# A decoder block on one core: the first sum of a job postponed, products cut into single pieces, and 26 of 64 steps plain instead of 30 in the last six jobs

## The chip, the core and the metric

The kernel runs on one core of a Trainium2 chip. The metric is the device time of one execution in microseconds (us); lower is better. The engines are called as in the profile: PE (TensorE, with PEld for its weight loads), DVE (VectorE), ACT (ScalarE), POOL (GpSimd) and SP (SyncE, which here only issues transfers).

## What is computed

A decoder block over 8 rows of 256 positions and 256 features, all in f32: two Mamba layers, cross attention, and a mixture of 8 experts of which each position uses 2. A layer norm closes each of the three. The two Mamba layers take most of the time. Their core is a recurrence over the positions, for 512 channels and 64 states each:

```python
def step(h, inp):
    u_t, dt_t, B_t, C_t = inp
    dA = jnp.exp(dt_t[:, :, None] * A)
    h = h * dA + (dt_t * u_t)[:, :, None] * B_t[:, None, :]
    y = jnp.einsum('bds,bs->bd', h, C_t)
    return (h, y)
...
combine = combine.at[jnp.arange(T)[:, None], topk_idx].set(topk_scores)
h = jax.nn.relu(jnp.einsum('td,ehd->teh', xf, w1) + b1)
expert_out = jnp.einsum('teh,edh->ted', h, w2) + b2
```

## The kernel before

A *job* is one Mamba layer of one row: 16 jobs, in the order of `JOBS` (row 0's first layer, then alternately the first layer of row b and the second of row b-1, at the end the second layer of row 7). A *step* is one of the 64 states of a job: all 512 channels (4 times 128 partitions) by 256 positions at once. There are 1024 steps, one after the other, and each passes four engines:

- PE fills `psX[i % 2]` with the input of step i (`fill_x`), after scan i-2 has left that buffer.
- ACT makes the decays `dA` with four exponentials (L1311).
- DVE runs the scan (L1343), a recurrence over 1024 elements, into `h`.
- POOL multiplies `h` by C (L1098) into `hC`, of which there are three.
- PE adds the result to `psY` with eight transposing matmuls (`sum_states`, L1656), two steps after (`LAG = 2`).

`KINDS` gives each step one of three ways to make its input. *Plain* (P): PE spreads b with 2 matmuls (L1619), and DVE multiplies by `dtu` in PSUM ahead of the scan (L1333). *Rows scaled* (T): ACT scales rows of `dtuT` (L1282) and PE turns them with 8 matmuls (L1627). *By matrix* (M): PE multiplies `dtuT` with a diagonal matrix in 16 matmuls (L1637); SP stores the diagonal nine steps ahead and loads the matrix five steps ahead. So P costs DVE an instruction, T costs ACT two, and M costs PE the most. Jobs 1 to 9 follow `EARLY` (22 P, 21 M, 21 T), jobs 10 to 15 follow `LATE`.

When the 64 states of a job are summed, DVE multiplies `psY` with the gate (`gate`, L1358), and only then may the first sum of the next job overwrite `psY`. In iteration i the instructions stand in this order: on PE `fill_x(i + 1)`, the sum of step i-2, then small work; on DVE the gate (where step i-2 is the first of a job), the multiplication of step i+1 if plain, the scan of step i+1.

*Small work* is all the rest: the projections, convolution and softplus of the next job, `turn` and `next` or `proj` behind the gate (L1762, L1595), attention, routing, and the experts in 53 tiles of 128 slots (`x_turn`, `hid` at L1595, `out` at L1682). The class `Schedule` plans it once, when the program is built: it keeps a model time for each engine, and after each step's own work `fill` takes tasks out of four chains (`chains`, rank 0 the next job, 1 a row's attention and routing, 2 experts, 3 outputs) as long as they end before `latest` says that the next fill, decay or product is due. A task is put at a step, `beside[i]`, and each engine does its pieces of `beside[i]` in that order. The first `WINDOW` tasks of each chain are looked at. A product of four matmuls is two tasks here (`z` and `z+`, `2 * MM` each), a fourth of a `hid` half is one of 448 ns. DVE takes small work only ahead of a plain step. Where the expert chain has nothing and room is left, `keep_busy` puts in `keep` pieces: `KEEP` = 4 times `TURN` = 109 ns of room is taken for each idle transpose (L1881). Whatever is not placed by the last step goes into `tail`; the experts of the last group (15 tiles, rows 6 and 7) always do, since row 7 must be routed first.

The planner's model of the sum does not wait for the gate.

Of the kernel before, what the change touches and what calls it, by code (L numbers as in the profile page):

```python
# [20 lines left out]
P = 128  # L21
# [31 lines left out]
LATE = "PTPMPTPTPMTPTPT" * 4 + "PTPM"  # L53
# [19 lines left out]
def kind_of(i):  # L73

    return KINDS[i] if 0 <= i < STEPS else PLAIN

# [33 lines left out]
WINDOW, FIRST, LONG, HOP = 24, 1500, 3300, 60  # L110
# [15 lines left out]

def task(name, n, part, eng, ns, *needs, opens=None, frees=None):
    return Task((name, n, part), eng, ns, needs, opens, frees)

# [11 lines left out]
def tasks_pre(n):  # L141
# [5 lines left out]
    if n >= 2:  # L147
        before = (("next+", n - 2, 1),) if JOBS[n - 2][0] == 0 else (("proj+", JOBS[n - 2][1], 1),)
    gates, out = [], []
    for tc in range(KL):  # L150
        gates += [task("z", n, tc, "PE", 2 * MM, *src, *((("u+", n, 1),) if n == 0 else ()), opens="G"),
                task("z+", n, tc, "PE", 2 * MM, ("z", n, tc)),
                task("z_copy", n, tc, "ACT", EVICT, ("z+", n, tc), frees=("z", n, tc))]
    if n > 0:
        out += gates
    for half in range(2):
        out += [task("u", n, half, "PE", 2 * MM, *src, *before, opens="G"),
                task("u+", n, half, "PE", 2 * MM, ("u", n, half))]
        if n == 0 and half == 1:
            out.append(task("conv", n, half, "DVE", 3600, ("u+", n, half), frees=("u", n, half)))  # L160
            continue
        for j in range(TAPS):
            needs = [("u+", n, half)]
# [9 lines left out]
    if n == 0:  # L173
        out += gates
    out += [task("silu", n, 0, "ACT", 4800, ("z_copy", n, 1), ("add_tap", n, (1 if n else 0, TAPS - 1)), *(() if n else (("conv", 0, 1),))),
            task("c", n, 0, "PE", 2 * MM, ("silu", n, 0), opens="G"),
            task("c+", n, 0, "PE", 2 * MM, ("c", n, 0)),
            task("c_copy", n, 0, "ACT", 400, ("c+", n, 0), frees=("c", n, 0)),
            task("b", n, 0, "PE", 8 * TURN, ("silu", n, 0), opens="G"),
            task("b+", n, 0, "PE", 8 * TURN, ("b", n, 0)),  # L180
            task("bT_copy", n, 0, "ACT", 330, ("b+", n, 0), frees=("b", n, 0))]
    for half in range(2):
        chain = (("log", n, 0),) if half else ()
        out += [task("dt", n, half, "PE", 2 * MM, ("c_copy", n, 0), opens="G"),
                task("soft", n, half, "ACT", 2 * EVICT, ("dt", n, half), *chain, frees=("dt", n, half)),
# [14 lines left out]
def tasks_post(n):  # L200
# [6 lines left out]
    if l == 0:  # L207
        out += [task("next", n, 0, "PE", 2 * MM, *copied, opens="G"),
                task("next+", n, 0, "PE", 2 * MM, ("next", n, 0)),
                task("next", n, 1, "PE", 2 * MM, ("next+", n, 0)),  # L210
                task("next+", n, 1, "PE", 2 * MM, ("next", n, 1)),
                task("next_copy", n, 0, "ACT", EVICT, ("next+", n, 1), frees=("next", n, 0))]
    else:
        out += [task("proj", b, 0, "PE", 2 * MM, *copied, opens="G"),
                task("proj+", b, 0, "PE", 2 * MM, ("proj", b, 0)),
                task("proj", b, 1, "PE", 2 * MM, ("proj+", b, 0)),
                task("proj+", b, 1, "PE", 2 * MM, ("proj", b, 1)),
                task("resid1", b, 0, "DVE", 2350, ("proj+", b, 1), frees=("proj", b, 0)),
                task("rstd", b, 0, "POOL", 900, ("resid1", b, 0)),
                task("norm1", b, 0, scaler(b), 780, ("rstd", b, 0))]  # L220
# [3 lines left out]
def tasks_kv(b):  # L224

    out = []
    for name, before in (("k", ("score+", b - 1, 0)), ("v", ("av+", b - 1, 0))):
        out += [task(name, b, 0, "PE", 2 * MM, *((before,) if b else ()), opens="G"),
                task(name + "+", b, 0, "PE", 2 * MM, (name, b, 0)),
# [4 lines left out]
def tasks_row(b):  # L234
# [7 lines left out]
    if b > 0:  # L242
        last.append(("b2_add", b - 1, 0))
# [1711 lines left out]
```

## Time and profile before

| | |
|---|---|
| time, median of 3 runs | 3259.71 us (3256.25 to 3264.41) |
| the profiled execution | 3258.22 us |
| its span, first to last instruction | 3256.4 us |
| its granted TensorE clock, mean | 0.970 |
| first scan to last scan | 35 to 3041 us |
| the last six jobs | 1854 to 3041 us |
| after the last scan | 215 us |

How to read it: each engine works from its own queue in order, and "idle" is the time in front of an instruction in which its engine did nothing; the name behind the arrow is what ended that. A group is all instructions of a line, engine and shape; its busy time is a union, the mean is that of one. PE's ends are modelled, so that matmuls behind each other overlap a little; the distance between the starts of two groups tells what a group costs PE.

### The profile page before, as it was taken

What the parts mean: (1) busy time and instruction counts of PE and PEld (TensorE: products, weight loads), DVE (VectorE), ACT (ScalarE), POOL (GpSimd) and SP (SyncE); (2) the same over time, 40 slices, a digit from 0 to 9 for tenths busy, and PEclk for the clock granted to TensorE, in tenths of its full rate; (3) what the DMA queues carried; (4) which work ended last, traced back from release to release, by engine and by line L of the source; (5) the groups of instructions that cost most, each with busy time, mean ns of one, the idle gap of its engine ahead of it and who ended that gap; (6) DMA issues with size and microseconds to landing.
All of it is one profiled execution on the core that took longest, in us unless ns stands there. A gap on an engine that the chain in (4) does not pass through costs nothing.

```text
span 3256.4 us, 59741 instructions
## 1 busy us (share of the span) xinstructions
PE 2873.5 (88%) x21945; PEld 2614.9 (80%) x21945; DVE 2911.1 (89%) x2039; ACT 2625.0 (81%) x6098; POOL 2661.3 (82%) x1317
## 2 busy tenths in 40 slices
PE   6889899998988899898988799899998989899676
PEld 5888888887878788787878789788888878888466
DVE  6999999999999999999999999999999999999410
ACT  7878888886879788887989699898989879788222
POOL 4989999898989899888989798887888788878401
PEclk8999999999999999999999999999999999999788
DMA  3345442222222222122222235334353335634076
GB/s 113 103 155 172 152 154 65 71 67 70 73 63 64 62 73 75 55 66 72 70 69 63 85 129 166 96 106 156 119 159 102 102 122 163 204 123 141 25 270 210
DMA packets 285448, 358.35 MB, mean 110 GB/s; under 512 B 100554, under 2 KB 180435, under 8 KB 284772
## 3 DMA queue, kind: packets, MB, share of 16 engines
q1 hardware_dynamic: 281202, 343.75, 33.7%
q0 software_dynamic: 3072, 8.39, 0.8%
q8 instruction: 175, 2.87, 0.4%
q10 hardware_dynamic: 882, 2.38, 0.2%
q14 instruction: 117, 0.96, 0.1%
HBM read 303.70 MB, written 50.73 MB: 109 GB/s over the span
## 4 chain that ended last, share of the span: by engine, by line
PE 32%; ACT 21%; POOL 17%; DVE 14%; issue 13%; DMA 2%; SPq 1%; POOLq 0%; DVEq 0%; ACTq 0%
POOL hC L1098 14%; ACT dA L1311 10%; PE psY L1656 9%; DVE h L1343 9%; PE psG L1595 8%; PE psX L1637 4%; ACT xs L1282 3%; PE psG L1682 3%; PE psX L1627 3%; DVE psX L1333 3%; PE psX L1595 2%; ACT gT L1153 1%; PE psX L1619 1%; DMA w_up<-in_w_exp 1%; ACT scratch L1150 1%
## 5 line engine op out<-in xcount | busy, mean ns | idle before, releaser
L1098 POOL TENSOR_TENSOR hC<-h,cb 128x1024 f32<-128x1024 f32 x1024 | 2401.9, 2368 | 376.7 <-DVE h L1343 361.2
L1343 DVE TENSOR_TENSOR_SCAN h<-dA,psX 128x1024 f32<-128x1024 f32 (+1 forms) x1102 | 2300.2, 2124 | 102.3 <-ACT dA L1311 34.0
L1311 ACT ACTIVATE dA<-dt,negA 128x255 f32<-128x255 f32 x4096 | 1722.3, 506 | 167.0 <-DVE h L1343 165.8
L1656 PE MATMUL psY<-ident,hC 128*128 128x128 f32 x8192 | 1087.5, 277 | 53.6 <-DVE gT L1358 39.4
L1656 PEld LDWEIGHTS psY<-ident,hC 128*128 128x128 f32 x8192 | 941.6, 143 | 69.5 <-DVE gT L1358 42.7
L1637 PE MATMUL psX<-diag_b,dtuT 128*128 128x128 f32 x4080 | 514.5, 280 | 52.1 <-DVE h L1343 49.2
L1637 PEld LDWEIGHTS psX<-diag_b,dtuT 128*128 128x128 f32 x4080 | 487.9, 195 | 86.3 <-issue 82.0
L1333 DVE TENSOR_TENSOR psX<-dtu,psX 128x1024 f32<-128x1024 f32 x411 | 497.0, 1209 | 22.2 <-PE psX L1619 21.6
L1627 PE MATMUL psX<-ident,xs 128*128 128x128 f32 x2864 | 382.0, 277 | 108.6 <-ACT xs L1282 66.9
L1282 ACT ACTIVATE xs<-dtuT,bT 128x512 f32<-128x512 f32 x716 | 477.0, 720 | 0.2
L1627 PEld LDWEIGHTS psX<-ident,xs 128*128 128x128 f32 x2864 | 320.6, 142 | 164.3 <-ACT xs L1282 91.1
L1682 PE MATMUL psG<-w_down,hid 128*128 128x256 f32 x692 | 180.2, 384 | 13.3 <-DMA w_down<-in_w_exp 6.1
L1619 PE MATMUL psX<-ident,bT 128*128 128x128 f32 x822 | 163.7, 282 | 15.1 <-DVE h L1343 13.1
L1595 PE MATMUL psG<-xgT,w_up 128*128 128x128 f32 x1216 | 164.8, 278 | 9.5 <-DMA w_up<-in_w_exp 6.0
L1595 PEld LDWEIGHTS psG<-xgT,w_up 128*128 128x128 f32 x1216 | 151.7, 192 | 19.3 <-DMA w_up<-in_w_exp 7.6
L1881 PE MATMUL psG<-ident 128*128 128x128 f32 x985 | 158.3, 273 | 0.0
L1682 PEld LDWEIGHTS psG<-w_down,hid 128*128 128x128 f32 x692 | 119.7, 191 | 31.9 <-DMA w_down<-in_w_exp 10.0
L1619 PEld LDWEIGHTS psX<-ident,bT 128*128 128x128 f32 x822 | 104.4, 141 | 49.0 <-DVE h L1343 26.7
L1881 PEld LDWEIGHTS psG<-ident 128*128 128x128 f32 x985 | 117.6, 141 | 4.8 <-issue 4.1
L1554 DVE SCALAR_TENSOR_TENSOR hC<-got,slot_weight,hC 128x256 f32<-128x256 f32 x8 | 3.7, 483 | 126.0 <-DMA got<-y_slots,slot_of 92.6
L1266 ACT ACTIVATE hid<-psG,b_tile 128x128 f32<-128x128 f32 x304 | 86.0, 370 | 31.5 <-PE psG L1595 31.4
L1054 POOL DMA_INDIRECT got<-y_slots,slot_of x28 | 29.1, 1040 | 92.2 <-DMA y_slots<-yg 86.5
(203 smaller groups left out, 2046.1 us busy)
## 6 DMA issues: line engine op xcount, KB each, us to landing
cb<-c_dram SPq DMA_DIRECT2D x256, 512.0 KB, 4.0
w_up<-in_w_exp SPq DMA_DIRECT2D x173, 256.0 KB, 3.1
w_down<-in_w_exp SPq DMA_DIRECT2D x173, 256.0 KB, 2.8
diag_b<-b_dram SPq DMA_DIRECT2D x255, 128.0 KB, 3.6
x_slots<-got SPq DMA_DIRECT2D x32, 512.0 KB, 5.0
y_slots<-got SPq DMA_DIRECT2D x32, 512.0 KB, 5.0
dA<-in_w_exp SPq DMA_DIRECT2D x39, 256.0 KB, 5.1
h<-in_w_exp SPq DMA_DIRECT2D x39, 256.0 KB, 4.9
```

Of the source, the lines that this page charges most:

```text
L1098: eng.tensor_tensor(hC[i % NHC][:, :, :], h[i % NH][:, :, :], cw.to_broadcast([P, KI, L]), ALU.mult).then_inc(times_c, 1)
L1282: made = eng.activation(xs[:, tc, :], dtuT[n % 2][:, tc, :], ACT.Identity, scale=bT[n % 2][:, tc, s:s + 1])
L1311: made = eng.activation(dA[j % NA][:, c, 1:L], dt[n % 2][:, c, 1:L], ACT.Exp, scale=negA[:, JOBS[n][0], c, s:s + 1])
L1333: eng.tensor_tensor(x[:, :, :], dtu[n % 2][:, :, :], x[:, KI - 1:KI, :].to_broadcast([P, KI, L]), ALU.mult).then_inc(times_b, 1)
L1343: made = eng.tensor_tensor_scan(h[i % NH][:, part, :].rearrange("p c t -> p (c t)"), dA[i % NA][:, part, :].rearrange("p c t -> p (c t)"), ...
L1595: made = eng.matmul(dst, lhs, rhs, start=begin and i == 0, stop=end and i == len(terms) - 1)
L1619: made = eng.transpose(psX[i % 2][:, KI - 1, tc * P:(tc + 1) * P], bT[n % 2][:, tc, s:s + 1].to_broadcast([P, P]), ident[:, :])
L1627: made = eng.transpose(psX[i % 2][:, c, tc * P:(tc + 1) * P], xs[:, tc, c * P:(c + 1) * P], ident[:, :])
L1637: made = eng.matmul(psX[i % 2][:, c, tc * P:(tc + 1) * P], dtuT[i // S % 2][:, tc, c * P:(c + 1) * P], diag_b[k % NDIAG][:, tc, :], start= ...
L1656: made = eng.matmul(psY[:, tc, c * P:(c + 1) * P], hC[i % NHC][:, c, tc * P:(tc + 1) * P], ident[:, :], start=s == 0 and c == 0, stop=s == ...
L1682: made = eng.matmul(bank[k][:, 0:D], hid[half][:, i, :], w_down[slot][:, i % 2, :], start=half == i == 0, stop=half == 1 and i == 3, skip_ ...
L1881: eng.transpose(bank["M"][:, 0:P], ident[:, :], ident[:, :])
```

## The change

Three edits.

1. `sums_at(i)`: the first sum of a job (but for job 0) is not done in iteration i = first step + 2, but in the next one, ahead of that iteration's own sum. The sums stay in the same order. The planner's model has the same.
2. `CUTS` and `cuts`: each product is planned, and may be done, in pieces of one matmul with 256 columns (a `hid` quarter in two of 224 ns, `o` in three per half, `logit`, `b2`, `dt`, `count` in two) instead of two pieces of two. The matmuls are the same and as many. `WINDOW` goes from 24 to 40, since the chains have more tasks.
3. `LATE`: 26 P, 25 T, 13 M instead of 30 P, 25 T, 9 M. The last step of all is P in both, so that the last job goes from 31 P and 8 M to 26 P and 13 M.

```diff
-LATE = "PTPMPTPTPMTPTPT" * 4 + "PTPM"
+LATE = "PTMPT" * 12 + "PTMP"
...
+def sums_at(i):
+
+    j = i - LAG
+    if j < 0 or j >= S and j % S == 0:
+        return ()
+    return (j - 1, j) if j > S and j % S == 1 else (j,)
...
-WINDOW, FIRST, LONG, HOP = 24, 1500, 3300, 60
+WINDOW, FIRST, LONG, HOP = 40, 1500, 3300, 60
...
+CUTS = {"z": 4, "u": 4, "c": 4, "b": 4, "dt": 2, "next": 4, "proj": 4, "k": 4, "v": 4, "q": 4, "score": 4, "av": 4, "o": 3,
+        "logit": 2, "b2": 2, "count": 2, "hid": 2}
...
+def cuts(name, n, part, ns, *needs, opens="G"):
+
+    first = task(name, n, part, "PE", ns, *needs, opens=opens)
+    return [first] + [task(name + "+" * i, n, part, "PE", ns, (name + "+" * (i - 1), n, part)) for i in range(1, CUTS[name])]
...
-        out += [task("u", n, half, "PE", 2 * MM, *src, *before, opens="G"),
-                task("u+", n, half, "PE", 2 * MM, ("u", n, half))]
+        out += cuts("u", n, half, MM, *src, *before)
...
-                out.append(task("hid", t, (half, i), "PE", HID_MM, ("xg_copy", t, 0), *before, opens=None if i else "M"))
+                out += cuts("hid", t, (half, i), HID_MM // 2, ("xg_copy", t, 0), *before, opens=None if i else "M")
...
             for i in range(STEPS + LAG):
-                j = i - LAG
                 if i + 1 < STEPS:
                     fill_x(i + 1)
-                if j >= 0:
+                for j in sums_at(i):
                     if 0 <= j % S - SKIP_FROM < KL * KI:
                         add_skip(j // S, *divmod(j % S - SKIP_FROM, KI))
                     sum_states(j)
```

The other lines of the diff carry the new pieces through the code that plans and issues each product.

## Rows read from the trace of the kernel before

**Rows 1.** The page, busy time of each engine over the span

```profile
PE 2873.5 (88%) x21945; PEld 2614.9 (80%) x21945; DVE 2911.1 (89%) x2039; ACT 2625.0 (81%) x6098; POOL 2661.3 (82%) x1317
```

**Rows 2.** Timeline, three steps P, M, T without small work

```profile
1503.16 0.38 PE L1619 MATMUL psX<-ident,bT 128*128 128x128 f32 x2
1503.38 1.04 PE L1656 MATMUL psY<-ident,hC 128*128 128x128 f32 x8
...
1505.35 2.02 PE L1637 MATMUL psX<-diag_b,dtuT 128*128 128x128 f32 x16 [0.94 <-DVE h L1343]
...
1506.36 6.64 DVE L1343 TENSOR_TENSOR_SCAN h<-dA,psX 128x1024 f32<-128x1024 f32 x3
...
1507.21 1.03 PE L1656 MATMUL psY<-ident,hC 128*128 128x128 f32 x8
```

**Rows 3.** Busy time by stretch: header, last six jobs, the tenth job, after the scans

```profile
core 0: us, PE busy (x) PEld busy (x) DVE busy (x) ACT busy (x) POOL busy (x), PEclk, DMA share, GB/s
1854.10:3041.00 1186.90, 1086.13 (x8281) 1000.50 (x8279) 1128.59 (x808) 1022.83 (x2455) 1000.79 (x491) 0.98 0.42 133
...
1854.10:2036.60 182.50, 172.10 (x1352) 160.66 (x1351) 178.94 (x98) 167.97 (x404) 163.17 (x77) 0.99 0.46 150
...
3041.00:3133.00 92.00, 51.56 (x195) 38.47 (x196) 17.07 (x66) 12.19 (x35) 12.40 (x12) 0.66 0.28 93
```

**Rows 4.** Groups by line, last six jobs: busy us, mean ns, idle before

```profile
L1333 DVE TENSOR_TENSOR psX<-dtu,psX 128x1024 f32<-128x1024 f32 x180 | 217.9, 1211 | 18.8 <-PE psX L1619 18.3
...
L1637 PE MATMUL psX<-diag_b,dtuT 128*128 128x128 f32 x848 | 105.6, 279 | 4.3 <-DVE h L1343 4.3
...
L1881 PE MATMUL psG<-ident 128*128 128x128 f32 x78 | 10.8, 273 | 0.0
```

**Rows 5.** Waits, last six jobs: who for whom, us, times, longest

```profile
PE psX L1627 <- ACT xs L1282: 30.3, 20, 5.0
...
DVE h L1343 <- PE psX L1627: 8.8, 11, 2.7
...
DVE h L1343 <- issue: 5.9, 4, 2.3
```

**Rows 6.** Waits, jobs 1 to 9

```profile
DVE h L1343 <- ACT dA L1311: 24.3, 32, 1.6
...
DVE h L1343 <- PE psX L1637: 13.0, 15, 2.2
```

**Rows 7.** Timeline, the border between job 0 and job 1

```profile
224.53 1.26 DVE L1358 TENSOR_TENSOR gT<-psY,sz 128x512 f32<-128x512 f32 x2
...
225.85 1.59 PE L1656 MATMUL psY<-ident,hC 128*128 128x128 f32 x8 [2.85 <-DVE gT L1358]
...
227.24 1.06 PE L1762 MATMUL psG<-ident,gT 128*128 128x128 f32 x4
...
228.31 2.62 PE L1637 MATMUL psX<-diag_b,dtuT 128*128 128x128 f32 x16
...
230.96 2.29 DVE L1343 TENSOR_TENSOR_SCAN h<-dA,psX 128x1024 f32<-128x1024 f32 x1 [1.71 <-PE psX L1637]
```

**Rows 8.** Timeline, the border between jobs 5 and 6, and that before job 15

```profile
1131.77 1.09 PE L1656 MATMUL psY<-ident,hC 128*128 128x128 f32 x8 [2.47 <-DVE gT L1358]
...
1132.88 6.64 DVE L1343 TENSOR_TENSOR_SCAN h<-dA,psX 128x1024 f32<-128x1024 f32 x3
...
2848.78 1.97 PE L1656 MATMUL psY<-ident,hC 128*128 128x128 f32 x8 [3.35 <-DVE gT L1358]
...
2852.91 1.23 DVE L1333 TENSOR_TENSOR psX<-dtu,psX 128x1024 f32<-128x1024 f32 x1 [2.00 <-PE psX L1619]
```

**Rows 9.** Busy time by stretch, behind the gate of rows 7 (columns as rows 3)

```profile
225.80:231.00 5.20, 5.15 (x32) 5.15 (x33) 3.46 (x3) 2.67 (x6) 3.20 (x2) 0.67 0.04 13
```

**Rows 10.** Chain of waits in order of time, two tiles of the tail

```profile
3144.71 3.57 PE psX L1595 x32
...
3151.96 3.57 PE psX L1595 x32
```

More of the change, by code:

```diff
@@ L240, in then, with then_cuts @@
         last[:] = [(name, b, part)]
+    def then_cuts(name, part, ns, *needs, opens="G"):
+        out.extend(cuts(name, b, part, ns, *needs, *last, opens=opens))
+        last[:] = [(last_cut(name), b, part)]
     if b > 0:
@@ L274, in tasks_row @@
     then("weights", 0, "DVE", 1000)
-    then("count", 0, "PE", 1300, opens="G")
+    then_cuts("count", 0, HID_MM)
     then("place", 0, "DVE", 1200, frees=("count", b, 0))
@@ L955, in small_work @@
                         load_tile(n)
-                    elif name in ("hid", "out") and part[1] % 2 == 1:
+                    elif name in (last_cut("hid"), "out") and part[1] % 2 == 1:
+                        name = name.rstrip("+")
                         used[name] = PAIRS * n + 2 * part[0] + part[1] // 2 + 1
@@ L1771, in small_work @@
                         made = product(dst[:, part * L:(part + 1) * L],
-                                       [(w_out[:, 0, c, part * P:(part + 1) * P], g[:, c, :]) for c in (2 * i, 2 * i + 1)], not second, second)
-                        if part == i == 1:
+                                       [(w_out[:, 0, i, part * P:(part + 1) * P], g[:, i, :])], i == 0, ends)
+                        if part == 1 and ends:
                             made.then_inc(full[k], 1)
@@ L1818, in small_work @@
                         dst = bank[k][:, part * D:(part + 1) * D]
-                        product(dst, [(ones_row[:, :], bo_row)], end=False)
-                        evicted(("av", n, 0))
-                        made = product(dst, [(qT[:, d, part * P:(part + 1) * P], w_att[:, WO, d, :]) for d in range(KD)], begin=False)
-                        if part == 1:
+                        if i == 0:
+                            product(dst, [(ones_row[:, :], bo_row)], end=False)
+                        else:
+                            evicted(("av", n, 0))
+                            made = product(dst, [(qT[:, i - 1, part * P:(part + 1) * P], w_att[:, WO, i - 1, :])], False, ends)
+                        if part == 1 and ends:
                             made.then_inc(full[k], 1)
@@ L1861, in small_work @@
                     elif name == "hid":
[L1862 to L1864 removed]
+                        half, c = part
+                        q = PAIRS * n + 2 * half + c // 2
+                        if c == i == 0:
                             open_bank((name, n, part))
```

187 lines of the change are left out of this document (89 added, 98 removed).

## The prediction

> **What bounds the kernel now.** I read the page first: DVE is the busiest engine, with PE one per cent behind it [rows 1], and both shares are means over a loop and a tail. Then the timeline of a stretch without small work. There the scans stand back to back: three of them take 6.64 us, so 2.21 us each, a plain step adds its multiplication of 1.21, and no engine makes DVE wait [rows 2, 4]. So in the loop DVE sets the pace, and each wait of DVE is a loss. The table by stretch says how tight this is in the last six jobs: DVE is busy 1128.6 of 1186.9 us, PE 1086.1, and job 10 has only 10 us of idle PE in 182.5 [rows 3]. Groups and waits tell who makes DVE late there: PE, with 18.3 us ahead of the multiplication [rows 4], 8.8 ahead of a scan of kind T, and 5.9 without a named releaser [rows 5], 33.0 in all. In jobs 1 to 9 ACT's decays cost more (24.3 us) than PE's matrices (13.0) [rows 6]; nothing of this change touches the decays. After the last scan PE works through the experts of the last group, 7.25 us per tile from start to start [rows 10], and waits much before that.
>
> **Part 1: fewer plain steps.** Five late jobs lose 4 plain steps and the last one 5, so 25 multiplications of 1.211 us leave DVE's queue [rows 4]: -30.3 us, as long as DVE stays the engine that is waited for. This count is exact. What takes their place is 25 more matrix steps. On PE a matrix fill costs the distance from its start to that of the next sum, 1.86 us, a plain one 0.22 [rows 2]: +1.64 each, +41 us in six jobs. That work is on no path as long as it fits: a matrix step needs 1.86 and a sum of at most 1.04 in a scan of 2.21, so it must start on time and leaves PE up to 0.7 late, and a plain step behind it gives that back, with 3.42 us of DVE for at most 1.26 of PE. In the new pattern each matrix step has a plain one behind it. Each T also has a P before it, so ACT's two scalings have that longer step to hide in; their number stays. SP gets 25 more stores and loads of matrices, five steps or some 13 us ahead of use. No row shows PE waiting for a matrix; the whole 5.9 us without a releaser is the upper bound of what such loads cost now, and doubled it is +6; I take nothing.
>
> **Part 2: the room on PE.** Idle PE in the six jobs is 1186.9 - 1086.1 = 100.8 us. It loses 41 to the fills and 30.3 to the shorter loop, and gets back 10.8 of idle transposes [rows 3, 4]: 40 us stay idle, 3.5% of 1157. Now PE waits 30.3 us for ACT's scaled rows alone [rows 5], and such waits come back. So I expect that not all expert tiles fit. How many: each of the 78 idle transposes stands for 436 ns of room that the planner had left, 34 us; the new need is 41 + 30 = 71; the missing 37 us are 5 tiles of 7.25, less what finer pieces recover. The planner does not make steps late for them, they go to the tail. There PE is idle 92.0 - 51.6 = 40.4 us while row 7 goes through attention and routing [rows 3], which is room for five tiles. Bounds: 0 if all fit or hide, +36 if five are paid in full. The nearer row is the idle one, but a tile in a hole also delays row 7's own products, so I take +6 for the tail, and +2 for more late fills in the loop, where PE is packed closer.
>
> **Part 3: the first sum.** At a border the gate follows the last-but-one scan, PE's queue stands 2.85 us in front of the first sum, and behind that are the turn (L1762) and the fill of step 4, a matrix. Sum, turn and fill end 5.1 us after the gate, the scan could have begun 3.5 us after it: it waits 1.71 [rows 7]. Ten of 15 borders show such a wait, from 1.71 at the first to 2.00 at the last, together 13.2 us; at the border before job 6 the sum took 1.09 us, no turn followed, and the scans ran on without any wait [rows 8]. The change puts the fill ahead of the sum, so that what the sum takes leaves this path: from 1.09 to 1.97 us [rows 8], never more than the wait itself, about 1.0 at ten borders, -10. It does not leave the queue: two sums then stand in front of the fill of step 5, which gives some back. I take -9, between 0 and -13.2. POOL waits for the first sum only three steps later. The gate waits for the last sum of the old job, which doesn't move.
>
> The granted clock belongs to this part. Behind that idle time the 5.2 us stretch has a mean of 0.67 [rows 9], a stretch partly at 1.2 and partly at 2.4 GHz, and the first sum takes 1.59 or 1.97 us where it takes 1.09 elsewhere [rows 7, 8]. If `turn` stays in front of the fill, as the planner may leave it (its sum does not wait for the gate in the model, and the turn does), PE stays idle as long as now and its clock still falls.
>
> The Trainium skill, TensorE: Matmul & The Clock Gate, section Part 1: The HAM clock gate, says that the engine is throttled by default and that activity releases it. By that, work in place of the idle time would give back the slow part too and this term would be nearer to -13; the trace agrees that the clock is down after the idle time.
>
> **Part 4: single pieces.** The work on PE is the same, only where it can be split changes. At most it takes away the waits for PE that are not at borders: 33.0 us in the late jobs less 6.4 at their borders, and in the early ones 13.0 for matrices [rows 6] less 6.9, so some 33 us. Late waits mostly stand behind expert pieces, of which `out` stays whole and `hid` is halved. The other bound is a loss, since the whole order changes: +10, a repeat of a third of today's late waits. Near the row of today's order I take -4.
>
> **The sum**, against the profiled execution of 3258.2 us, which is 1.5 under the median: -30.3 + 6 + 2 - 9 - 4 = -35.3, so 3223 us. Head and tail are otherwise as before: the product pieces of the tail run back to back either way.
>
> A rule that speaks to part 2: the Trainium skill, Perfetto Trace Analysis, section Identifying the Most-Contended Engine, holds that matmul busy time misstates TensorE's headroom and that weight-load busy time is the better measure. In the late jobs that is 1000.5 of 1186.9, 84% against 91.5%. By it far more than 40 us would stay free and the +8 would be near 0, giving 3215. I go by the starts in the timeline, since they say what each fill costs the queue.
>
> **Rivals.**
>
> A, PE becomes the bound in the late jobs. For it: 3.5% of idle time is left, and in job 10, where PE had 94%, the new work of 4 x 1.64 us is more than the 5.6 that stay idle in a job shorter by 4.8. Against it: the fills come first in PE's order and only experts have to give way. If waits for PE double from 27 to 54 us in the late jobs and the rest is as above, the time is 3223 + 25 = 3248.
>
> B, slower than before. The place is the same, the end of the loop and the tail: the tiles that don't fit hold up the routing of row 6 and the outputs behind it, and row 7 starts its attention late. Its price is 7.25 us per tile. It decides from the point where more tiles are paid in full than the 35 us hold, that is beyond five, on top of the waits of A. With A and five tiles paid: 3248 + 36 - 6 = 3278. Against it: 40.4 us of idle PE in the tail and 34 us of unused room today.
>
> C, single pieces do what they can: two thirds of the 33 us go instead of 4, and all tiles hide, so 3223 - 18 - 6 = 3199; with part 3 at its own end 3195.
>
> D, the postponed sum doesn't do what it says: the turn in front of the fill keeps PE waiting for the gate, the slow clock stays, and the sum only moves its 1.04 us to the next step. Then 3223 + 9 = 3232.
>
> **How the numbers follow.** The forecast 0.50 (own range 3212 to 3236); D 0.12; C 0.14; A 0.16; B 0.08. A measurement of this kernel can tell about 0.3%, 9.8 us, from no change. Faster by more (under 3249.9): the forecast, D, C and half of A, 0.84; within 0.3%: most of the rest of A, 0.08; slower: B, 0.08. The range takes in C and A's middle: 3195 to 3250. It leaves out B, the upper end of A and the far end of C.
>
> **What would show it.** L1333 with 25 instructions fewer, L1637 with 400 matmuls more. The last six jobs shorter by 30 to 40 us. At the borders: the wait ahead of the scan or multiplication of step 4 gone or under 0.9 us, L1637 or L1627 in front of two L1656 groups, and PE's idle time in front of L1656 for the gate much under 2.85 us. Idle transposes gone from job 15, and more than 15 tiles of L1682 after the last scan, with PE busier than 51.6 us there. PE's idle time in the late jobs at 40 us or a little more. The prediction is wrong if waits of DVE for PE in the late jobs rise over 33 us by as much as part 1 gives, if the stretch after the last scan grows by more than 20 us, or if ACT's decays (24.3 us in the early jobs) start to set the end of late steps.

## The result, and the profile after

The changed kernel is slower: 3289.12 us (median of 4 runs, 3285.00 to 3296.95) against 3258.38 (4 runs, 3256.25 to 3264.41), a ratio of 1.0091 [1.0077, 1.0104]. The forecast was 3223 with a range of 3195 to 3250, so the time lies outside, on the other side of no change. The profiled execution took 3286.5, its span 3284.7.

The first view to read is busy time by stretch, cut at the end of the last scan: once for all work, and once for the products `out` of the experts alone, of which a tile has 16 matmuls. Changed kernel first (columns as rows 3):

```profile
core 0: us, PE busy (x) PEld busy (x) DVE busy (x) ACT busy (x) POOL busy (x), PEclk, DMA share, GB/s
1852.70:3006.20 1153.50, 1050.71 (x8071) 973.25 (x8070) 1089.33 (x736) 994.96 (x2354) 986.37 (x476) 0.98 0.37 116
3006.20:3284.70 278.50, 220.89 (x1377) 197.76 (x1374) 43.49 (x137) 81.92 (x268) 37.73 (x39) 0.91 0.71 240
...
1852.70:3006.20 1153.50, 112.00 (x434) 75.13 (x435) 0.98 0.37 116
3006.20:3284.70 278.50, 97.22 (x414) 75.20 (x414) 0.91 0.71 240
```

The same two stretches of the kernel before:

```profile
3040.80:3256.40 215.60, 150.02 (x852) 129.95 (x852) 29.07 (x100) 52.18 (x166) 22.85 (x23) 0.80 0.55 186
...
1854.10:3040.80 1186.70, 159.73 (x608) 104.57 (x608) 0.98 0.42 133
3040.80:3256.40 215.60, 58.62 (x240) 44.46 (x240) 0.80 0.55 186
```

The loop did what was wanted: its last scan ends at 3006.2 instead of 3040.8 (-34.6 us), and the last six jobs take 1153.5 instead of 1186.7. But the stretch behind it grew from 215.6 to 278.5 (+62.9). Of the 848 `out` matmuls 414 stand behind the last scan instead of 240, which is 174 / 16 = 10.9 tiles more; in the loop there are 434 instead of 608. And PE's idle time in the last six jobs, 1153.5 - 1050.7 = 102.8 us, is not 40 as forecast, but about the 100.6 that it was before.

The sum is about the same, but the idle time has other owners. First the groups by line, then the waits (who for whom, us, times, longest), both of the last six jobs:

```profile
L1350 DVE TENSOR_TENSOR psX<-dtu,psX 128x1024 f32<-128x1024 f32 x155 | 187.3, 1209 | 5.3 <-PE psX L1636 5.1
...
L1654 PE MATMUL psX<-diag_b,dtuT 128*128 128x128 f32 x1248 | 161.9, 285 | 20.4 <-DVE h L1360 19.8
```

```profile
PE psX L1644 <- ACT xs L1299: 34.3, 26, 4.7
...
PE psX L1654 <- DVE h L1360: 19.8, 36, 1.5
DVE h L1360 <- ACT dA L1328: 17.1, 20, 3.1
DVE h L1360 <- PE psX L1644: 13.5, 10, 5.7
DVE h L1360 <- PE psX L1654: 11.6, 11, 2.3
```

155 multiplications instead of 180, and 1248 matrix matmuls instead of 848, as planned. PE waits for ACT's scaled rows a little longer than in [rows 5], 34.3 against 30.3. And 36 matrix fills are at the head of PE's queue before the scan that frees their buffer has ended: 19.8 us, where the kernel before had 4.3 in six. Little of either reaches DVE: of these 62 waits five stand ahead of a fill that DVE then waited for, 3.4 us in all. But each is time in which no expert piece runs, since in PE's queue it stands behind the fill. The gate, for which PE waited 14.0 us here before, has now 4.6. So that the two sums come out alike, 100.6 and 102.8, is in part chance.

### The profile page after: what moved, and what is told of

It is laid out like the page before. It is cut to its first block, busy times and chain, and to the rows that moved or that the text cites. A ratio compares the mean times of both kernels' runs of the same rounds, so it can differ in the third digit from the quotient of the medians.

```text
span 3284.7 us, 60520 instructions
## 1 busy us (share of the span) xinstructions
PE 2909.5 (89%) x22305; PEld 2673.8 (81%) x22305; DVE 2885.6 (88%) x2004; ACT 2626.9 (80%) x6098; POOL 2660.5 (81%) x1317
## 4 chain that ended last, share of the span: by engine, by line
PE 31%; ACT 20%; DVE 18%; POOL 15%; issue 12%; DMA 2%; SPq 1%; POOLq 0%; DVEq 0%; ACTq 0%
POOL hC L1115 13%; DVE h L1360 12%; ACT dA L1328 9%; PE psY L1673 8%; PE psG L1612 7%; PE psX L1654 6%; DVE psX L1350 4%; ACT xs L1299 4%; PE psX L1644 3%; PE psX L1699 2%; PE psX L1612 1%; PE psG L1699 1%; ACT gT L1170 1%; ACT scratch L1167 1%; DMA w_down<-in_w_exp 1%
## 5 line engine op out<-in xcount | busy, mean ns | idle before, releaser
L1360 DVE TENSOR_TENSOR_SCAN h<-dA,psX 128x1024 f32<-128x1024 f32 (+1 forms) x1092 | 2301.0, 2143 | 114.5 <-ACT dA L1328 39.4
L1654 PE MATMUL psX<-diag_b,dtuT 128*128 128x128 f32 x4480 | 570.8, 282 | 70.6 <-DVE h L1360 67.4
L1654 PEld LDWEIGHTS psX<-diag_b,dtuT 128*128 128x128 f32 x4480 | 538.7, 195 | 109.3 <-issue 105.0
L1350 DVE TENSOR_TENSOR psX<-dtu,psX 128x1024 f32<-128x1024 f32 x386 | 466.4, 1208 | 13.2 <-PE psX L1636 12.7
L1612 PE MATMUL psG<-xgT,w_up 128*128 128x128 f32 x1088 | 153.1, 282 | 12.8 <-DMA w_up<-in_w_exp 8.7
L1636 PE MATMUL psX<-ident,bT 128*128 128x128 f32 x772 | 152.4, 280 | 13.1 <-DVE h L1360 11.4
L1612 PEld LDWEIGHTS psG<-xgT,w_up 128*128 128x128 f32 x1088 | 141.6, 196 | 19.8 <-DMA w_up<-in_w_exp 10.1
L1902 PE MATMUL psG<-ident 128*128 128x128 f32 x867 | 136.7, 273 | 0.0
L1699 PE MATMUL psG<-w_down,hid 128*128 128x256 f32 x496 | 127.2, 383 | 10.5 <-DMA w_down<-in_w_exp 9.7
L1636 PEld LDWEIGHTS psX<-ident,bT 128*128 128x128 f32 x772 | 96.7, 140 | 39.4 <-DVE h L1360 22.5
L1699 PEld LDWEIGHTS psG<-w_down,hid 128*128 128x128 f32 x496 | 86.3, 190 | 23.5 <-DMA w_down<-in_w_exp 12.7
L1902 PEld LDWEIGHTS psG<-ident 128*128 128x128 f32 x867 | 102.8, 141 | 1.2 <-issue 0.7
```

What stands on the lines that cost most here:

```text
L1350: eng.tensor_tensor(x[:, :, :], dtu[n % 2][:, :, :], x[:, KI - 1:KI, :].to_broadcast([P, KI, L]), ALU.mult).then_inc(times_b, 1)
L1360: made = eng.tensor_tensor_scan(h[i % NH][:, part, :].rearrange("p c t -> p (c t)"), dA[i % NA][:, part, :].rearrange("p c t -> p (c t)"), ...
L1612: made = eng.matmul(dst, lhs, rhs, start=begin and i == 0, stop=end and i == len(terms) - 1)
L1636: made = eng.transpose(psX[i % 2][:, KI - 1, tc * P:(tc + 1) * P], bT[n % 2][:, tc, s:s + 1].to_broadcast([P, P]), ident[:, :])
L1654: made = eng.matmul(psX[i % 2][:, c, tc * P:(tc + 1) * P], dtuT[i // S % 2][:, tc, c * P:(c + 1) * P], diag_b[k % NDIAG][:, tc, :], start= ...
L1699: made = eng.matmul(bank[k][:, 0:D], hid[half][:, i, :], w_down[slot][:, i % 2, :], start=half == i == 0, stop=half == 1 and i == 3, skip_ ...
```

## What the stretch after the last scan costs

Here is PE's own timeline of that stretch in the changed kernel, tiles being turned (`x_turn`, L1880):

```profile
3089.37 0.38 PE L1880 MATMUL psX<-ident,xg 128*128 128x128 f32 x2
...
3097.41 0.38 PE L1880 MATMUL psG<-ident,xg 128*128 128x128 f32 x2
...
3122.40 0.38 PE L1880 MATMUL psG<-ident,xg 128*128 128x128 f32 x2
...
3130.44 0.38 PE L1880 MATMUL psX<-ident,xg 128*128 128x128 f32 x2
...
3138.48 0.38 PE L1880 MATMUL psX<-ident,xg 128*128 128x128 f32 x2
```

and of the kernel before, POOL's last send of row 7 and the first tile of the last group:

```profile
3104.09 0.97 POOL L1045 DMA_INDIRECT x_slots<-x,slot_of  x1 [0.30 <-issue]
...
3108.70 0.69 PE L1859 MATMUL psG<-ident,xg 128*128 128x128 f32 x2 [7.66 <-DMA xg<-x_slots]
```

Before, the last group (tiles 38 to 52) starts 67.9 us after the last scan, 4.6 us after the last send of row 7, and PE had been waiting for it. In the changed kernel that send is at 83.5, but tiles 32 to 37 of the group before go through PE first, most of them 8.04 us apart, and tile 38 is turned at 3138.48, 132.2 us after the last scan. From there to the end both kernels need about as long, 147.7 and 146.3 us. So +64.3 at the start of the last group is the +62.9 of the tail. The two rows of this stretch say the same by PE's account: it is busy 70.9 us longer (220.9 against 150.0) and idle only 8.0 less (57.6 against 65.6). One piece of idle time is new, right behind the turn of tile 38: ACT, which must copy it, first waits for the store of an earlier result (`yg`), which SP issues behind ten loads.

```profile
3142.05 0.38 SPq L868 DMA_DIRECT2D y_slots<-yg  x1
...
3147.60 0.38 ACT L1290 ACTIVATE yg<-psX 128x256 f32<-128x256 f32 x1 [11.23 <-DMA y_slots<-yg]
...
3148.31 3.78 PE L1612 MATMUL psG<-xgT,dA 128*128 128x128 f32 x16 [9.45 <-ACT xgT L1271]
```

The following table, read from such timelines, has this for every kernel that says something on it (us after its last scan; `resid1` is the sum behind `proj` with which row 7 begins its attention).

| kernel | tiles finished after the last scan | `resid1` of row 7 | last send of row 7 | tile 38 turned | tail |
|---|---|---|---|---|---|
| before | 15 | 16.1 | 63.3 | 67.9 | 215.6 |
| changed | 25.9 | 41.2 | 83.5 | 132.2 | 278.5 |
| tiles_held_back | 26 | 14.3 | 56.5 | 129.2 | 274.3 |
| turned_instead | 21.4 | 64.0 | 102.8 | 107.9 | 254.6 |
| turned_gate_first | 21.4 | 10.8 | 49.8 | 84.7 | 231.3 |
| sum_mixed_153 | 20.9 | 35.8 | 74.6 | 82.0 | 225.7 |
| mixed_gate_first | 20.9 | 14.1 | 56.9 | 85.2 | 230.2 |

## The experiments

Ratios are against the kernel before, run beside each on the same chip; in brackets the 95% interval. "Tail" is the time after the last scan of the profiled execution.

**Is it the pattern, or the sum and the pieces?** The changed kernel with the old `LATE`; and the kernel before with the new one:

```diff
-LATE = "PTMPT" * 12 + "PTMP"
+LATE = "PTPMPTPTPMTPTPT" * 4 + "PTPM"
```

> The changed kernel with the step pattern of before (30 plain steps in each late job), so the postponed first sum and the single pieces alone. Theory: the loss lies in the pattern alone, which takes room from PE that expert tiles then lack. Without it the two other edits give what the borders and finer pieces give, 5 to 12 us under the kernel before, ratio 0.996 to 0.9985, and 15 tiles stand after the last scan. Rival: single pieces or the postponed sum cost something themselves (a new order of small work, two sums in a row), then it is 5 us or more over the kernel before.

> The kernel before with the new pattern alone. Theory: the loop gets 20 to 30 us shorter and the stretch after it 50 to 70 us longer, ratio 1.007 to 1.015, a little slower than the full change. Rival: the loss needs the single pieces (many half products that fill the gaps while whole ones wait); then this one is faster than the kernel before, ratio 0.990 to 0.997.

old_pattern took 3259.92 us, 1.0003 [0.9993, 1.0014], with a tail of 212.9. pattern_alone took 3301.50, 1.0121 [1.0102, 1.0140], with 24.7 tiles after the last scan and a tail of 272.4. The loss is the pattern's, and the other two edits together are worth nothing with the old one. Two expectations were missed: old_pattern did not gain 5 to 12 us, and the loop of pattern_alone ended only 14.5 us earlier (3026.3), not 20 to 30.

**Are the tiles the cost?** The changed kernel without 11 of the 15 tiles of the second group (they are not computed, and so its time is not that of the whole work); and the kernel before, whose planner may not put tiles 27 and up into the loop:

```diff
+TILES[1] -= 11
```

```diff
                 for t in chain[:WINDOW]:
+                    if rank == 2 and t.piece[1] >= 27 and t.piece[0] != "tile_out":
+                        break
```

> The changed kernel, but of the second group's 15 expert tiles only 4 are computed, so that nothing of the first two groups need be left for the tail; its output lacks those experts. Theory: what the change lost is the tiles after the loop, and with 11 fewer of them the loop keeps its 35 us of gain and the tail falls back from 278 to about 216 us, which gives 3220 to 3232 us. Rival: the tail is long for another reason (outputs of six rows instead of three, late loads), then the time stays over 3250.

> The kernel before, with tiles 27 to 37 of the second group held back from the loop, so that 26 tiles instead of 15 stand after the last scan; the steps and their pattern are as before. Theory: each tile costs the tail 5 to 7 us although PE has 40 us of idle time there, so the tail grows by 50 to 75 us; the loop gets a few us shorter, total 3300 to 3325. Rival (the step of the prediction): five of the tiles hide in the idle time before row 7 is routed, and the tail grows by 44 us or less, total 3285 to 3300.

eleven_tiles_less took 3219.46, 0.9880 [0.9862, 0.9897]: with 15 tiles left, the time is the one forecast for the whole kernel. tiles_held_back took 3309.86, 1.0157 [1.0140, 1.0173]. The stretch after the last scan, all work and then `out` alone, of tiles_held_back, and under it of eleven_tiles_less:

```profile
3033.60:3307.90 274.30, 223.34 (x1407) 199.10 (x1406) 31.25 (x104) 84.72 (x276) 27.15 (x27) 0.90 0.71 237
...
3033.60:3307.90 274.30, 97.72 (x416) 76.61 (x416) 0.90 0.71 237
```

```profile
3001.00:3214.00 213.00, 148.73 (x860) 129.51 (x860) 43.37 (x136) 52.29 (x166) 37.78 (x39) 0.81 0.60 203
...
3001.00:3214.00 213.00, 58.51 (x240) 44.41 (x240) 0.81 0.60 203
```

With the old pattern, the old sum and the old pieces, 11 tiles more behind the loop cost the same as in the changed kernel: a tail of 274.3 against 278.5. In return the loop got only 7.2 us shorter (3033.6 against 3040.8): in the loop these 11 tiles had cost next to nothing. What they had filled shows as idle PE, 155.3 us in the last six jobs in place of 100.6:

```profile
1854.90:3033.60 1178.70, 1023.39 (x7650) 934.61 (x7649) 1126.57 (x803) 996.27 (x2345) 996.65 (x486) 0.97 0.36 112
```

So a tile is nearly free in the loop and costs 5.3 us on average behind it (58.7 / 11).

**What the other two edits do.** sum_alone is the kernel before with `sums_at` of the change. pieces_alone is the changed kernel with the old `LATE` and without the postponement; pattern_and_pieces is the changed kernel without the postponement; pattern_and_sum is sum_alone with the new `LATE`. Without the postponement means:

```diff
-    if j < 0 or j >= S and j % S == 0:
-        return ()
-    return (j - 1, j) if j > S and j % S == 1 else (j,)
+    return (j,) if j >= 0 else ()
```

> The kernel before with the postponed first sum alone. Theory: the borders get up to 9 us less of waits by the prediction's step, but both edits together gave nothing on the old pattern, so what a border gives back is lost within the next steps: within 3 us of the kernel before. Rival: the sum gives its 5 to 9 us and the single pieces take them away again, ratio 0.997 to 0.9985.

> The kernel before with the products in single pieces and the longer window of the planner alone. Theory: no difference, within 3 us. Rival: they cost what the sum gives, ratio 1.0015 to 1.003.

> The changed kernel with the first sum in its old place: new pattern and single pieces. In its plan 19 tiles stand after the last step, against 23 with the postponed sum and 22 with the pattern alone. Theory: the time follows the tiles left over, at 5 to 6 us each; with four fewer and a loop some 10 us longer it takes 3270 to 3285 us, less than the change. Rival: the postponed sum is worth its part at the borders, then it is 3290 us or more.

> The kernel before with the new pattern and the postponed sum, products in whole pieces. The plan leaves 19 tiles, against 22 for the pattern alone. Theory: time follows the tiles: 3 fewer at 5 to 6 us and the sum's own 10 us, so 3272 to 3285 us, less than the changed kernel with its 23. Rival: single pieces are what makes the new pattern bearable; then it is 3290 us or more.

sum_alone took 3251.55, 0.9967 [0.9954, 0.9979], a gain of 0.33%, some 10 us. pieces_alone took 3264.50, 1.0013 [1.0004, 1.0023], a loss of 4. On the new pattern it looks different: with the pieces it is 1.0062 [1.0048, 1.0077], with the sum 1.0083 [1.0062, 1.0103], alone 1.0121, with both (the changed kernel) 1.0091. So beside the pattern alone the pieces are worth 0.6% (24.7 tiles left become 23.3), and beside pattern and sum nothing (24.0 become 25.9). The sum, added to pattern and pieces, costs about 0.3%, with intervals that just touch: 23.3 tiles were left before it and 25.9 with it, and the loop ends earlier (3006.2 for 3017.9). That the shorter loop takes away the room in which tiles stood fits this and is not shown. On the old pattern the two edits do not add either: alone they would make 0.9980, together they measure 1.0003. Why is open. Of the four expectations only that of pattern_and_pieces was met; pattern_and_sum was to take at most 3285 us, sum_alone to change nothing, and pieces_alone lies between its forecast (within 3 us) and its rival (1.0015 or more).

What the sum does at a border, first in the changed kernel (border between job 0 and 1, to be read beside [rows 7]), then in sum_alone:

```profile
229.99 0.66 PE L1778 MATMUL psG<-ident,gT 128*128 128x128 f32 x4 [2.85 <-DVE gT L1375]
...
230.59 1.95 PE L1654 MATMUL psX<-diag_b,dtuT 128*128 128x128 f32 x16
...
231.10 6.64 DVE L1360 TENSOR_TENSOR_SCAN h<-dA,psX 128x1024 f32<-128x1024 f32 x3
232.38 1.91 PE L1673 MATMUL psY<-ident,hC 128*128 128x128 f32 x16
```

```profile
228.55 0.76 PE L1771 MATMUL psG<-ident,gT 128*128 128x128 f32 x4 [2.85 <-DVE gT L1367]
...
229.32 3.41 PE L1646 MATMUL psX<-diag_b,dtuT 128*128 128x128 f32 x16
```

The sum has left the path, but at this border the turn now stands at the head of the queue and waits for the gate the same 2.85 us. It is so at six of the 15 borders of the changed kernel; over all 15 PE's idle time for the gate falls from 39.4 us to 21.7 (19.7 in sum_alone), and DVE's waits for PE behind the gate from 13.2 to 4.2 (2.6). After the same idle time the fill of 16 matmuls took 1.95 us in one kernel and 3.41 in the other.

**Is there room that the planner only does not use?** If its margin ahead of a fill is what keeps PE idle, half of it should fill the holes:

```diff
-MARGIN = {"PE": 300, "ACT": 300, "POOL": -600}
+MARGIN = {"PE": 150, "ACT": 300, "POOL": -600}
```

> The changed kernel with the planner's margin ahead of PE's fills at 150 ns instead of 300. The plan leaves 18 tiles instead of 23 for the tail and has a loop 28 us longer. Theory: the margin holds a good part of the idle time, so tiles come back into the loop, but as waits of DVE: idle PE falls from 103 to under 85 us, the tail by 25 us or more, the loop grows by 20 to 30 us, and the time is 3275 to 3295 us. Rival: the idle time comes from waits for scans and scaled rows and not from the margin; then idle PE stays over 95 us.

3286.32 us, 1.0088 [1.0071, 1.0105]: nothing gained on 1.0091. PE's idle time in the last six jobs stays at 99.6, and all of DVE's waits there rise from 53.0 to 65.2. Three tiles did come back into the loop (23.0 are left) and the tail is 14.7 us shorter, but the loop is 16.3 us longer, and both cancel. So it is not this margin that holds the room; no other value of the planner's model was tried.

**Which patterns leave room?** Five runs change what follows what. six_patterns is the changed kernel with a pattern of its own for each late job (170 plain steps, 144 with rows scaled, 70 by matrix). The others stand on sum_alone. sum_28plain and turned_instead repeat one pattern:

```diff
-LATE = "PTPMPTPTPMTPTPT" * 4 + "PTPM"
+LATE = "TPTPMTPTPTPTPMTPTPTPTPMTPTPTPTPTMPTPTPTPTMPTPTPTPTMPTPTPTPTMPTPT"
...
+LATE = "TPTPMTPTPTPTMTPTPTPTPTMPTPTPTMTPTPTPTPTMTPTPTPTPTMPTPTPTMTPTPTPT"
```

sum_mixed has six patterns with 27, 30, 26, 29, 26, 29 plain steps, and sum_mixed_153 has these, with 29, 26, 24, 22, 24, 28:

```diff
+LATES = ["PTMPTPTPMTPTPMPTPTPTMPTPTPMPTPTPMTPTPMPTPTPMTPTPMTPPTPTMPTPTPMTP",
+         "PTMPTPTMPTPTMPTPTMPTPTMPTPTMPTPTMPTPMTPTPMTPTPMTPTPMTPTPMTPTPMTP",
+         "TPMTPMTPTPMTPTPMTPMTPTPMTPTMPTPTMPTPMTPTMPTPTMPTMPTPTMPTPTMPTMPT",
+         "PMTPMTPMTPMTPMTPMTPMTPMTPMTPMTPMTPMTPMTPMTPMTPMTPMTPMTPMTPMTPMTP",
+         "TPMTPMTPTPMTPTPMTPMTPTPMTPTMPTPTMPTPMTPTMPTPTMPTMPTPTMPTPTMPTMPT",
+         "PTMPTPTPMTPTPTMPTPTPMPTPTMPTPTPTMPTPTPMTPTPMPTPTPMTPTPTMPTPTPMTP"]
-KINDS = FIRST_JOB + EARLY * 9 + LATE * (NJ - 10)
+KINDS = FIRST_JOB + EARLY * 9 + "".join(LATES)
```

> The two other edits of the change with a pattern of its own for each late job: 30, 30, 29, 27, 22 and 32 plain steps of 64, 170 instead of 181 in all, chosen so that the plan leaves no more than the last group's 15 tiles for the tail. Theory: plain steps can go only where no tile is pushed out; 11 fewer are worth 13 us, so 3245 to 3252 us, faster than both kernels. Rival: the tighter steps give it back as waits of DVE, then 3256 us or more.

> The kernel before with the postponed first sum and 28 plain, 29 turned and 7 matrix steps in each late job, spread evenly; the plan leaves the last group's 15 tiles alone for the tail. Theory: 12 multiplications fewer are worth 14.5 us only if no tile is pushed out and DVE's waits don't grow; with the sum's 10.7 that would be 3236 us; half of it lost to waits gives 3243, ratio 0.992 to 0.995. Rival: as with six patterns, closer packing gives all of it back as waits, then it is no better than the sum alone, ratio 0.9965 or more.

> The kernel before with the postponed first sum and 26 plain, 31 turned and 7 matrix steps in each late job: as few plain steps as the change, but turned in place of matrix steps, which take 0.87 us of PE instead of 1.86. Theory: the room on PE decides; 24 fewer plain steps cost it some 30 us for the shorter loop, and the fills hardly more than before, so only 2 to 4 tiles are pushed out instead of 11, 3250 to 3265 us. Rival: what decides is the number of plain steps (DVE takes small work only ahead of them) or ACT's load; then it is as slow as with 13 matrices, 3280 us or more.

> The kernel before with the postponed first sum and a pattern of its own for each late job: 27, 30, 26, 29, 26 and 29 plain steps, 167 in all, still with 15 tiles for the tail in the plan. Theory: the planner's gain is lost as waits of DVE, as with six patterns: 3245 to 3255 us. Rival: the single pieces were at fault there; then 3232 to 3240 us.

> The kernel before with the postponed first sum and 29, 26, 24, 22, 24 and 28 plain steps in the late jobs, 153 in all, three fewer than the change; the plan leaves 18 tiles for the tail instead of the change's 23. Theory: the order of the steps costs the room more than their number, so with these orders the loop is as short as the change's and only 3 tiles more than before stand behind it, 3225 to 3245 us. Rival: with so few plain steps the tiles go out as in the change, over 3265 us.

| kernel | plain steps in six jobs | us, ratio | PE idle there | tiles after the last scan |
|---|---|---|---|---|
| before | 181 | 3258.38 | 100.6 | 15 |
| changed | 156 | 3289.12, 1.0091 | 102.8 | 25.9 |
| six_patterns | 170 | 3258.90, 0.9986 [0.9976, 0.9995] | 92.3 | 15.3 |
| sum_28plain | 169 | 3244.91, 0.9942 [0.9924, 0.9960] | 92.7 | 15 |
| turned_instead | 157 | 3258.90, 0.9994 [0.9983, 1.0005] | 105.6 | 21.4 |
| sum_mixed | 167 | 3236.67, 0.9931 [0.9912, 0.9950] | 74.0 | 16 |
| sum_mixed_153 | 153 | 3226.69, 0.9908 [0.9892, 0.9925] | 67.2 | 20.9 |

turned_instead has as few plain steps as the changed kernel (one more) and pays for them on ACT instead of PE, whose fills of kind T need 8 matmuls and not 16. Beside pattern_and_sum, its counterpart with matrices, 1.0083 becomes 0.9994 and 24 tiles become 21.4, so PE's time for the fills seems a part of the loss (the order of the steps differs too). It is not all, since PE idles as long as ever, and 6.4 tiles went out where 2 to 4 were expected. sum_mixed_153 has fewer plain steps still and more matrix steps, 86 against 78, and yet leaves five tiles fewer behind, and PE is idle for 67.2 us instead of 102.8. It has the products in whole pieces; its nearest partner, pattern_and_sum, idles for 96.2 us and leaves 24.0. Its waits in the last six jobs:

```profile
PE psX L1642 <- ACT xs L1297: 18.2, 21, 2.7
...
PE psX L1652 <- DVE h L1358: 9.6, 15, 1.6
```

Both waits that the changed kernel's pattern has are about half as long (34.3 and 19.8 there; 34.8 and 26.1 in pattern_and_sum). All waits of PE for scaled rows or scans ahead of a fill tell the patterns apart: 44.5 us before, 61.5 in the changed kernel, 65.9 in turned_instead, 43.7 in sum_28plain, whose one pattern is spread evenly too, and 31.5, 35.3 and 33.2 in six_patterns, sum_mixed and sum_mixed_153.

six_patterns missed its forecast of 3245 to 3252 all the same: PE now waited for late weights of the experts (35.6 us, against 12.0 in the changed kernel; the row shows the larger of its two parts), and DVE's waits rose to 69.3 us and ate the shorter jobs. sum_mixed was expected to lose its gain in the same way and did not; it took what its rival said, that the single pieces were at fault in six_patterns. The two differ in their patterns as well, so the pieces' part in it is not shown.

```profile
PE psG L1705 <- DMA w_down<-in_w_exp: 24.1, 12, 6.0
```

**The number of tiles, or the gate held behind them?** In the last iterations the planner knows no next fill that could be late, and its limit is open. It puts expert pieces ahead of the last sums, and PE's queue runs them in that order, also when their weights are late. The changed kernel, just after its last scan:

```profile
3009.90 1.13 PE L1699 MATMUL psG<-w_down,hid 128*128 128x256 f32 x4 [1.31 <-DMA w_down<-in_w_exp]
...
3011.09 1.91 PE L1673 MATMUL psY<-ident,hC 128*128 128x128 f32 x16
...
3013.10 1.29 DVE L1375 TENSOR_TENSOR gT<-psY,sz 128x512 f32<-128x512 f32 x2 [6.86 <-PE psY L1673]
```

In two kernels the planner may not do that:

```diff
             for rank, chain in enumerate(self.chains):
+                if rank == 2 and limit["PE"] > 1e11:
+                    continue
                 for t in chain[:WINDOW]:
```

> As the kernel with 153 plain steps spread evenly and the postponed sum (3226.69 us), but in the last iterations, where the plan knows no limit for PE any more, no expert piece may be put in front of the last sums and the gate. The plan leaves 2 more tiles behind the loop. If the gate held behind expert pieces sets the end: resid1 goes from 35.8 us after the last scan to about 16 to 20, and the time falls by 5 to 10 us, to 3217 to 3222. If the count of leftover tiles sets the end: the pieces only move behind the gate, resid1 comes early, the last tile does not, and the time stays at 3223 to 3235.

> The same on the kernel with turned products in place of the four plain ones (3258.9 us), where the gate waited 32.4 us for expert pieces and resid1 stood 64.0 us after the last scan. The plan leaves 4 more tiles behind the loop. If the held gate sets the end: resid1 at about 16 to 20 us and a time of 3235 to 3245. If the count of tiles sets it: the tail counted from the last scan grows with the tiles while the loop ends earlier by the same work, and the time stays within 5 us of 3259.

mixed_gate_first took 3228.15, 0.9901 [0.9875, 0.9927], the same as its partner's 0.9908. turned_gate_first took 3239.24, 0.9939 [0.9918, 0.9959], against 0.9994: some 20 us gained. The gate behind the last scan, in turned_instead and then in turned_gate_first:

```profile
3036.14 1.29 DVE L1367 TENSOR_TENSOR gT<-psY,sz 128x512 f32<-128x512 f32 x2 [32.44 <-PE psY L1665]
```

```profile
3006.71 1.29 DVE L1369 TENSOR_TENSOR gT<-psY,sz 128x512 f32<-128x512 f32 x2 [3.69 <-PE psY L1667]
```

Both leave as many tiles behind the last scan as their partners (20.9 and 21.4). The two results look opposed and the table of the tail joins them. The last group can start when two things are done: row 7 is sent (plus some 5 us), and the tiles ahead of it are through PE. In turned_instead the first came last (102.8, start at 107.9), and with the gate first the tiles did (sent by 49.8, start at 84.7). In sum_mixed_153 both were close together (74.6 and 82.0), so there was nothing to win. In the changed kernel the tiles come last by far (83.5 and 132.2), so the held gate, which I see in its trace too, can cost it little by itself.

## Why the prediction was wrong, point by point

- **What bounds the kernel.** Right for the loop: DVE sets its pace. But PE's small work is bound to the loop only by being placed there, and the end by how much is left.
- **Part 1, right in mechanism; its size held in the changed kernel.** L1350 is run 386 times instead of 411, and the six jobs are 33.2 us shorter (1186.7 to 1153.5), near the 30.3 of the multiplications. DVE's waits for PE there stayed about the same, 30.2 us against 27.6; those for ACT's decays doubled, from 8.6 to 17.1. Jobs 1 to 9 became 5.5 us shorter (1636.1 to 1630.6), what stands ahead of them 4.1 longer (218.0 to 222.1). The size is no property of the pattern: in pattern_alone the same 25 multiplications made the six jobs only 16.3 us shorter (1170.4), and DVE's waits grew by 17.3 (46.7 to 64.0).
- **Part 2, the step that failed.** It counted idle PE as room: 100.8 - 41 - 30 + 11 = 40 us left, and five tiles at most that don't fit. Measured: 102.8 us idle and 10.9 tiles moved. PE's idle time in these jobs was between 93 and 109 us in every kernel with one repeated `LATE` that let all tiles compete, also where fills took 41 us more. The largest part of it is a queue in order that waits for its own fills, 44.5 of 100.6 us before ([rows 5] showed the largest) and 61.5 of 102.8 after; the rest is the gate, late weights of the experts, and small work that waits for ACT. The forecast said that such waits come back, and yet took most of them as used up. The work that the pattern and the shorter loop needed came out of the expert tiles. By PE's queue, from start to start and without the waits, expert pieces take 76 us less in the last six jobs (288 to 212), 7.0 per tile. Against that stand 44 more for fills of kind P and M (the forecast's 41), 7 more for other work, 33 less loop and 2 more idle time, less the 10 of idle transposes.
- **Part 2, its second half.** 6 us for up to five tiles behind the loop was not far off: the 5.9 extra tiles of sum_mixed_153 make the tail 10.1 us longer (225.7) and move the start of tile 38 from 67.9 to 82.0. What was wrong is the number of tiles, and what those beyond it cost: from sum_mixed_153 to the changed kernel five more tiles move that start by 50.2 us, some 10 each, more than the 7.25 of [rows 10]. And the 40.4 us of [rows 3] are not all ahead of the last group: up to the turn of tile 38 PE was idle for 32.5 us, and in the changed kernel for 23.2 still.
- **Part 3, the sum: right in size, partly wrong in how.** -9 forecast, -0.33% measured. PE's idle time for the gate went or became shorter at nine of the 15 borders; at six it moved in front of the turn, as D said. The gain came at both kinds, as the sum's own time left the path: DVE's waits for PE behind the gate fell by 9.0 us in the changed kernel. On top of the new pattern the same edit cost about 0.3%, which the forecast had no term for.
- **Part 4, single pieces.** -4 forecast, +4 measured alone [+1 to +8 by the interval], inside its bounds, with the wrong sign.
- **The rivals.** B was the one that came, by the part of its mechanism that says that tiles beyond those that the holes take are paid in full. The other part, that row 7 starts its attention late, did happen (41.2 us after the last scan for 16.1) but did not set the end: in tiles_held_back it starts at 14.3 and the tail is as long. Its 3278 is near the 3289 by luck: it holds 25 us for A, which did not come, and five paid tiles where there were more. I had set its chance at 0.08 because of 34 us of unused room (the 78 idle transposes) and of the idle PE in the tail. The changed kernel has no idle transpose in the last six jobs: that room was real, 10.8 us of busy time, and used. The rest was not used. A, waits of DVE for PE doubled, did not happen: 30.2 us for 27.6.
- **What I had asked of the profile.** "The stretch after the last scan grows by more than 20 us" was the sign that fell, by 62.9. The count of `out` matmuls behind the loop, which I named too, tells it in one row.
- **A page against the rows.** The Trainium skill, Perfetto Trace Analysis, section Identifying the Most-Contended Engine, judges TensorE's headroom by weight-load busy time (and by the share of peak work) and not by matmul busy time; by weight loads 16% were free in the last six jobs. The measured answer is that the changed kernel had no use even of the 8.5% that the matmuls' busy time leaves [rows 3]. With weight loads at 84% still (973.25 of 1153.5) eleven tiles went behind the loop.

What stays open: why exactly PE idles for 67 us in sum_mixed_153 and for 103 in the changed kernel. That its two largest waits are halved is shown. That the place of M straight behind T is the cause of the changed kernel's waits is only argued, and it can't be all: the pattern of before has no M behind a T, and PE idled for 100.6 us. Single pieces differ between the two as well. It is the planner's model that puts a tile into the loop or behind it, and of this model only one margin was tried; that another planner could not use more of the idle time is not shown. Whether the gate held for 6.86 us costs the changed kernel anything was not tried by itself, nor were the 9.45 us behind the turn of tile 38. And the effect of the six patterns was not tried apart from their lower count of plain steps, only beside kernels of other counts.

The best version found is sum_mixed_153: the kernel before with the postponed sum and six patterns of their own for the late jobs, with 153 plain steps, at 3226.69 us (3222.06 to 3230.05), 0.9908 [0.9892, 0.9925].

## What to carry to other kernels

Idle time of an in-order engine is room only where independent work can stand in front of the wait that makes it; find by name what each piece of it waits for before you subtract new work from it, and if the waits are those of the pattern itself, do not count on them as room until a run shows it. When work is moved from the bounding engine to its neighbour, ask what fills that neighbour's gaps today, where it goes, and what it costs there: here a tile cost next to nothing in the loop, 5.3 us on average behind it, and some 10 beyond the first six. An edit that shortens the loop is worth its gain only as long as what hides in the loop still fits, and single edits need not add.

## What the runs showed of the hardware

- The same idle time before the same fill gave two speeds. Behind 2.85 us without work, 16 matmuls of a fill took 1.95 us in the changed kernel and 3.41 in sum_alone. The stretch from the gate to the end of that fill, in the changed kernel and in sum_alone, has these granted clocks:

```profile
228.00:232.40 4.40, 2.41 (x22) 2.42 (x23) 4.37 (x5) 2.03 (x5) 3.47 (x2) 1.00 0.46 166
```

```profile
226.50:232.60 6.10, 4.05 (x22) 4.05 (x23) 5.42 (x5) 3.63 (x8) 3.54 (x2) 0.72 0.35 127
```

  The first is the 2.4 GHz level throughout, the second partly that of 1.2. Ahead of the idle time PE did the same in both: a fill of 8 matmuls, a sum, four idle transposes and a plain fill, at the same distances. So whether the clock falls at a border is not told by the length of the idle time alone. The Trainium skill, TensorE: Matmul & The Clock Gate, section Part 1: The HAM clock gate, has the engine throttled by default until activity releases it. At this border sum_alone agrees, its clock being down behind the idle time, and the changed kernel kept its clock through the same idle time.
- Tiles of the second last group are 8.04 us apart in PE's queue where those of the last are 7.25 [rows 10], with the same matmuls. Each of the first shows a wait of about 0.5 us for ACT's copy of the turned tile, most of the difference:

```profile
3098.32 3.84 PE L1612 MATMUL psX<-xgT,dA 128*128 128x128 f32 x32 [0.53 <-ACT xgT L1271]
```

  In the last group `out` products of the tile before stand between a turn and its first `hid`, and that wait is not seen.
